# Expert weights split into halves during attention and read back from DRAM, results scattered without addition, experts of the first 512 tokens chosen after the last attention block

## What is computed

```
def _route(x, gate_w, gate_bias):
    scores = sigmoid(x @ gate_w.T)                 # n x 16
    sb = scores + gate_bias
    group_scores = sum of the best 2 of sb in each of 4 groups of 4
    masked = sb where its group is one of the best 2 groups, else -inf
    tidx = the best 4 of masked
    w = scores[tidx] / (sum(scores[tidx]) + 1e-20) * 2.5
combine[n, tidx] = w
hact = silu(x @ w1[e].T) * (x @ w3[e].T) * combine
y = sum over e of hact @ w2[e].T
out = x + tanh(g) * (y + shared expert(x))         # 1024 tokens, experts of 256 x 192
```

## Time and profile before

| | |
|---|---|
| median of 3 runs | 1149.02 us (1147.89 to 1149.88) |
| the profiled execution's own time | 1146.89 us |
| its span, first to last instruction | 1145.1 us |
| granted TensorE clock, mean | 0.955 |
| busy share of the span | PE 86%, DVE 71%, ACT 63%, POOL 37% |
| after the last attention block (from about 921 us) | 224 us |

### The profile page before, as it was taken

How to read it: one execution, slowest core, us unless ns; L and a number is a source line. 1 busy time by engine, 2 the same in 40 slices (tenths; PEclk the granted TensorE clock), 3 DMA queues, 4 the chain that set the end, 5 groups by cost and what they waited for, 6 DMA issues and landing times. The chain is left out here.

```text
span 1145.1 us, 19033 instructions
## 1 busy us (share of the span) xinstructions
PE 988.5 (86%) x6544; PEld 872.5 (76%) x6544; DVE 818.6 (71%) x1655; ACT 723.5 (63%) x1393; POOL 419.6 (37%) x407
## 2 busy tenths in 40 slices
PE   1789989898799989999999999999999868279892
PEld 1668878687688768898888889898888867268882
DVE  6687765777623389897888889887888874666553
ACT  3477756766633478777777878777777743166551
POOL 5164432543167700402022020402017138666663
PEclk9899989999999999999999999999999888589996
DMA  4100000001211399300100001000002114467676
GB/s 132 33 1 1 1 5 1 1 1 38 78 42 35 111 278 281 114 1 2 37 1 1 1 1 38 1 1 2 29 1 69 48 41 143 137 162 129 104 116 139
DMA packets 70767, 67.51 MB, mean 59 GB/s; under 512 B 15505, under 2 KB 67985, under 8 KB 70161
## 3 DMA queue, kind: packets, MB, share of 16 engines
q1 hardware_dynamic: 62368, 55.66, 17.5%
q0 software_dynamic: 8304, 10.64, 5.7%
HBM read 34.20 MB, written 32.07 MB: 58 GB/s over the span
## 5 line engine op out<-in xcount | busy, mean ns | idle before, releaser
L337 PE MATMUL PS<-R 128*128 128x512 f32 (+3 forms) x2669 | 576.4, 360 | 44.3 <-POOL R L562 8.2
L337 PEld LDWEIGHTS PS<-R 128*128 128x128 f32 x2669 | 429.4, 195 | 102.2 <-issue 23.5
L1713 DVE TENSOR_TENSOR R<-PS,R 128x512 fp32r<-128x512 f32 x320 | 205.0, 682 | 40.0 <-ACT R L1366 39.1
L1366 ACT ACTIVATE R<-PS 128x512 fp32r<-128x512 f32 x320 | 174.6, 596 | 79.8 <-PE PS L812 78.6
L1329 ACT ACTIVATE FA<-PS,nmax 128x1024 f32<-128x1024 f32 (+1 forms) x160 | 192.6, 1204 | 34.7 <-DVE nmax L1702 18.0
L825 PE MATMUL PS<-R 128*128 128x256 f32 x1408 | 203.7, 290 | 12.0 <-DVE FB L1721 10.7
L812 PE MATMUL PS<-eye,FA 128*128 128x128 f32 x1408 | 185.5, 276 | 12.5 <-DVE R L1713 4.2
L825 PEld LDWEIGHTS PS<-R 128*128 128x128 f32 x1408 | 179.7, 191 | 20.0 <-issue 17.3
L812 PEld LDWEIGHTS PS<-eye,FA 128*128 128x128 f32 x1408 | 161.2, 141 | 44.1 <-issue 19.6
L1702 DVE TENSOR_REDUCE nmax<-PS 128x1 f32<-128x1024 f32 x128 | 155.5, 1220 | 33.3 <-PE PS L337 22.9
L520 POOL TENSOR_SCALAR R<-R 64x512 fp32r<-64x512 f32 x40 | 25.8, 646 | 318.9 <-ACT R L1481 259.0
(11 more groups left out here) (249 smaller groups left out, 1240.0 us busy)
## 6 DMA issues: line engine op xcount, KB each, us to landing
rows<-xs SPq DMA_DIRECT2D x3, 5869.5 KB, 45.6
FA<-rows SPq DMA_DIRECT2D x47, 136.5 KB, 2.6
wst<-w_in SPq DMA_DIRECT2D x4, 1024.0 KB, 5.1
wst<-we_in SPq DMA_DIRECT2D x16, 256.0 KB
wst<-we_in SPq DMA_DIRECT2D x24, 128.0 KB
sums<-xs SPq DMA_DIRECT2D x2, 1152.0 KB, 23.3
FB<-k_in SPq DMA_DIRECT2D x16, 128.0 KB, 2.0
FA<-sums SPq DMA_DIRECT2D x8, 256.0 KB, 4.6
```

Of the source, the lines that this page charges most:

```text
L337: last = mm(out, a, b, start=(n == 0), stop=(n == len(passes) - 1), skip_group_check=skip)
L1366: a_(L.pt[0][:, (u // 2) % 2, 4 * g_:4 * g_ + 4, (u % 2) * P:(u % 2) * P + P], L.turn(u, g_).rearrange("p (t n) -> p t n", t=4), ACT.Copy) ...
L1713: inc(v.tensor_tensor(lo, turned, hi.bitcast(F32), ALU.subtract), "p_lo")
```

## The change

Four things change.

- **Weights.** During the second attention SP loads each raw expert (5 DMAs), POOL splits it in three pieces (`presplit`, two instructions each) and SP stores the two halves to a DRAM buffer `split_d`; two experts at a time, at fixed places of POOL's program. From the last block on POOL issues one DMA of 128 x 2560 values for each expert (`fetch_expert`), from float32 in DRAM to float32r in `R`, in six groups with a semaphore each. The splits by ACT, POOL and DVE after the attention go.
- **Results.** The weight of a choice is no longer multiplied in before the scatter. Every choice of every token has a DRAM row of its own in `parts_d` (4 x token + choice), so POOL's scatter is a plain one; 4 may be in flight. SP's load of rows no longer waits for it. At the end SP loads all four parts of 128 tokens (8 DMAs of 512 KB), and DVE adds them with their weights, 32 instructions.
- **Choice.** Chunk 0's groups are chosen after the block's outputs are split, its experts after the second sequence's norm; the rest follows with chunk 1, ahead of most of the shared expert.
- **Fill.** The zero rows are written in three parts between the loads of the experts; the two sum buffers are gone.

```diff
-PLANES = 2
+SPARE_ROWS = NB * S * 4
 CHUNKS = ((0, 4), (4, 4))
-SPLIT_POOL = 11
-HI_AT = {1: 9, 2: 10, 4: 11, 6: 12, 8: 13, 10: 14, 12: 15}
-LO_AT = {5: 11, 7: 12, 9: 13, 11: 14, 13: 15}
-LOAD_AT = {3: (9, 10), 7: (11, 12), 9: (13,), 11: (14,), 13: (15,)}
+FETCHED = ((0, 1, 2), (3, 4, 5), (6, 7, 8, 13, 14), (9, 10), (11, 12), (15,))
+FETCHED_IN = {e: i for i, group in enumerate(FETCHED) for e in group}
...
+    raw_gate_up, raw_down = FB[:, 1024:1792], xs[:, 0:512]
+    pieces = [(raw_gate_up[:, 0:512], 6144, 0), (raw_gate_up[:, 512:768], 9216, 512), (raw_down, 6144, 768)]
...
-    sums_d = [nc.dram_tensor(f"sums{i}", (NB * S + P, D), F32, kind="Internal").ap() for i in range(PLANES)]
+    parts_d = nc.dram_tensor("parts", (SPARE_ROWS + 48 * P, D), F32, kind="Internal").ap()
+    split_d = nc.dram_tensor("split", (E, P, WX), F32, kind="Internal").ap()
...
+        def stage_expert(e):
+            m, h = e // 2, e % 2
+            full, part, c = 2 + 3 * m + 2 * h, 3 + 3 * m, slice(DH * h, DH * h + DH)
+            gate_up = raw_gate_up.rearrange("p (a i) -> p a i", a=4)
+            cols = we_d[:, :, 0:512].rearrange("t p (a i) -> t p a i", a=4)
+            if e == 0:
+                sp.wait_ge(s["xc_lo"], 4)
+            first(sp, "e_split", 3 * e)
+            sp.dma_start(gate_up[:, :, 0:P], cols[full]).then_inc(s["raw_in"], 16)
+            sp.dma_start(gate_up[:, :, P:EI], cols[part][:, :, c]).then_inc(s["raw_in"], 16)
+            sp.dma_start(raw_down[:, 0:256], we_d[full][:, 512:768]).then_inc(s["raw_in"], 16)
+            for rows, _ in halves:
+                sp.dma_start(raw_down[rows, 256:512], we_d[part][c, 512:768]).then_inc(s["raw_in"], 16)
+            for i, (src, at, col) in enumerate(pieces):
+                n = src.shape[1]
+                sp.wait_ge(s["e_split"], 3 * e + i + 1)
+                sp.dma_start(split_d[e].rearrange("p (j c) -> p j c", j=2)[:, :, col:col + n],
+                             R[:, at:at + 2 * n].bitcast(F32).rearrange("p (j c) -> p j c", j=2)).then_inc(s[f"stored{i % 2}"], 16)
...
+        def preset_rows(c):
+            sp.wait_ge(s["preset"], 1)
+            sp.dma_start(rows_d.rearrange("(c p) n -> p c n", p=P)[:, c:c + 43, :],
+                         fill.unsqueeze(1).to_broadcast([P, 43, ROW])).then_inc(s["filled"], 16)
...
+        for g in range(1, NG1):
+            for e in range(4 * g - 2, 4 * g):
+                stage_expert(e)
+            if g < 3:
+                preset_rows(43 * g)
+            for e in range(4 * g, 4 * g + 2):
+                stage_expert(e)
+            if g + 1 < NG1:
+                sp.wait_ge(s["w1o_split"], g + 1)
+                sp.dma_start(wst[:, 0:W1_COLS], w1_d[g + 1]).then_inc(s["w1_in"], 16)
...
-                sp.wait_ge(s[f"sent{j % PLANES}"], 16 * ((j - HELD) // PLANES + 1))
+                sp.wait_ge(s["xt_done"], j - HELD + 1)
+                sp.wait_ge(s["dest_sum"], j - HELD + 1)
...
+        sp.wait_ge(s["weighted"], 1)
+        for r in range(RINGS):
+            sp.wait_ge(s[f"sent{r}"], 16 * len(range(r, TILES, RINGS)))
+        parts = parts_d[0:SPARE_ROWS, :].rearrange("(t p k) n -> t p (k n)", p=P, k=4)
+        for t in range(NB * TT):
+            sp.dma_start(back[t], parts[t]).then_inc(s[f"got{t}"], 16)
...
+        def presplit(e):
+            pool.wait_ge(s["raw_in"], 80 * (e + 1))
+            for i, (src, at, _) in enumerate(pieces):
+                n = src.shape[1]
+                first(pool, f"stored{i % 2}", 16 * (e if i == 1 else 2 * e + i // 2))
+                hi, lo = R[:, at:at + n], R[:, at + n:at + 2 * n]
+                g.tensor_scalar(hi, src, 1.0, 0.0, ALU.mult, ALU.add).then_inc(s["pool_free"], 1)
+                pool.wait_ge(s["pool_free"], 3 * e + i + 1)
+                g.tensor_tensor(lo, src, hi.bitcast(F32), ALU.subtract).then_inc(s["e_split"], 1)
+                pool.wait_ge(s["e_split"], 3 * e + i + 1)
...
+            presplit(4 * i - 2)
+            presplit(4 * i - 1)
...
+        def fetch_expert(e):
+            c = expert_at(e)
+            g.dma_start(R[:, c:c + WX], split_d[e]).then_inc(s[f"weights_in{FETCHED_IN[e]}"], 16)
+        pool.wait_ge(s["pj_done"], 28 * NG1)
         for e in range(3):
-            expert_split(e)
-        pool.wait_ge(s["rbc"], 2 * (2 * NG1 + 2))
-        pool.wait_ge(s["o_sum"], BLOCKS * (2 * NG1 + 2))
-        row_numbers(4, 4)
-        pool.wait_ge(s["at_lo"], 4 + 4 * NG1)
-        for h in range(2):
-            half = before16[:, 128 * h:128 * h + 128]
-            step(g.iota(half.bitcast(I32), [[1, 8], [-1, E]], base=8 * h, channel_multiplier=0))
-            step.wait()
-            step(g.tensor_scalar(half, half.bitcast(I32), 0.0, float(P), ALU.is_gt, ALU.mult))
-        step.wait()
-        pool.sem_inc(s["consts"], 1)
-        expert_lo(3)
-        expert_lo(4)
+            fetch_expert(e)
+        pool.wait_ge(s["scored"], UNITS * (2 * NG1 + 2))
+        for e in range(3, 6):
+            fetch_expert(e)
+        pool.wait_ge(s["pv_done"], BLOCKS * (2 * NG1 + 2))
+        for e in (6, 7, 8, 13):
+            fetch_expert(e)
+        pool.wait_ge(s["wo_done"], 4 + 4 * NG1)
+        fetch_expert(14)
...
         place_rows(0)
-        expert_lo(5)
-        expert_lo(6)
         place_rows(1)
+        pool.wait_ge(s["part_set"], 2)
         g.memset(hrow[:, :, EI:256], 0.0).then_inc(s["hrow_zeroed"], 1)
-        for e in range(7, SPLIT_POOL):
-            expert_lo(e)
+        pool.wait_ge(s["e_y"], 4)
+        for e in range(9, 13):
+            fetch_expert(e)
         for j in range(TILES):
-            plane = j % PLANES
+            r = j % RINGS
+            if j == 8:
+                pool.wait_ge(s["y_done"], 8)
+                fetch_expert(15)
+            pool.wait_ge(s["dest_set"], j + 1)
             pool.wait_ge(s["y_out"], j + 1)
-            if j >= PLANES:
-                pool.wait_ge(s[f"sent{plane}"], 16 * (j // PLANES))
-            g.indirect_dma_start(sums_d[plane],
-                                 bass.IndirectOffsetOnAxis(ap=got[:, j % HELD, ROW - 1:ROW].bitcast(U32), axis=0),
-                                 put[:, j % RINGS, :], None, compute_op=ALU.add).then_inc(s[f"sent{plane}"], 16)
+            if j >= RINGS:
+                pool.wait_ge(s[f"sent{r}"], 16 * (j // RINGS))
+            g.indirect_dma_start(parts_d, bass.IndirectOffsetOnAxis(ap=tile_dest[:, j:j + 1], axis=0), put[:, r, :],
+                                 None).then_inc(s[f"sent{r}"], 16)
...
+            if j < E:
+                group_of = FETCHED_IN[j]
+                pe.wait_ge(s[f"weights_in{group_of}"], 16 * len(FETCHED[group_of]))
...
-                elif u == 16:
-                    choose(0)
             attention(L1, b, C, fill)
             if not more:
                 out_norm(L1, C)
                 out_lo(L1, b, C)
-                find_slots(0)
+                choose_groups(0)
...
         norm(4 * NB + 2, x_tiles(1), late1)
+        choose_experts(0)
+        split_norm(3 * NB + 2, 1)
+        mark_chosen(0)
+        number_rows(0)
+        find_slots(0)
+        find_weights(0)
+        choose_groups(1)
+        choose_experts(1)
+        mark_chosen(1)
+        number_rows(1)
+        find_slots(1)
+        find_weights(1)
         job(0, 0)
         job_low(0, 0)
-        split_norm(3 * NB + 2, 1)
-        choose(1)
         job(1, 1)
-        find_slots(1)
         job_low(1, 1)
-        job(2, 0)
-        job_low(2, 0)
-        job(3, 1)
-        job_low(3, 1)
-        dve.wait_ge(s["consts"], 2)
+        dve.wait_ge(s["ew_split"], 2)
...
+        v.tensor_copy(owned[:, :, E], tile_iota)
+        job(2, 0)
+        job_low(2, 0)
+        do(v.tensor_tensor(owned[:, :, 0:E], owner[:, :, 0:E], owner[:, :, 1:E + 1], ALU.subtract))
+        job(3, 1)
+        job_low(3, 1)
...
-        def expert_lo(e):
-            dve.wait_ge(s["w_hi"], e - 2)
-            r, hi, lo = e % 2, expert_at(e), expert_at(e) + WX // 2
-            v.tensor_tensor(R[:, lo:lo + 768], raw_in[r], R[:, hi:hi + 768].bitcast(F32), ALU.subtract)
-            inc(v.tensor_tensor(R[:, lo + 768:lo + 1280], raw_out[r], R[:, hi + 768:hi + 1280].bitcast(F32), ALU.subtract),
-                "w_dve")
+        def find_shares():
+            total, inverse = bo[:, 200:208], bo[:, 208:216]
+            parts = part_w.rearrange("p (t k) -> p t k", k=4)
+            do(v.tensor_reduce(total, parts, AX.X, ALU.add))
+            do(v.tensor_scalar(total, total, 1e-20, None, ALU.add))
+            do(v.reciprocal(inverse, total))
+            do(v.tensor_scalar(inverse, inverse, 2.5, tg[:, 3:4], ALU.mult, ALU.mult))
+            inc(v.tensor_tensor(weight.rearrange("p (t k) -> p t k", k=4), parts,
+                                inverse.unsqueeze(2).to_broadcast([P, NT, 4]), ALU.mult), "weighted")
...
-            if j in LO_AT:
-                expert_lo(LO_AT[j])
-        for w in range(4):
```

(59 more changed lines are left out.)

233 lines of the change are left out of this document (78 added, 155 removed).

## The result

The changed kernel took **1141.98 us** (median of 6 runs, 1140.45 to 1143.81); the kernel before took 1149.45 in as many runs beside it. The ratio is 0.9929, 95% interval 0.9905 to 0.9954: 8 us faster (5 to 11), where the forecast of 1130 meant 19. The stated range was 1117 to 1150.

A forecast was written before the change was run, and what follows sets the result against it. It took the attention as PE-bound and the tiles as held by the pair of adds. Terms 0 − 24.4 + 1.5 − 4.5 + 9.1 = −18.3 gave span 1126.8, 1130.7 on the median's scale, told as 1130; range 1117 to 1150.

The forecast's parts named there:

- Part 2: Tile stage: sums' waits and splits between tiles go, PE sets the pace at 2.12 us a tile; −24.4 us.
- PE's floor of 2.08 us: Tile stage: spacing of two PE row turns where nothing was late, against 2.67 us each in the kernel before.
- what holds it is the pair of adds: Tile stage before: POOL waits 1.79 us for an earlier add; ACT and SP wait for the same landings.
- Parts 4 and 5: Kernel's end: last scatter's way to the return's loads −4.5 us; return with 4 MB instead of 2, +9.1 us.
- Part 6: Attention: presplits fit in POOL's room, 10 to 12 us each, the fill stays under the attention; 0 us.
- Cover that holds: Attention: query copies and low parts of keys queued behind presplits stay covered unless presplit DMAs take over twice the estimate.
- The mechanism stood among the rivals: Attention: POOL's presplit subtractions slow DVE beside them, late query copies hold PE; 10 to 20 us, 1140 to 1150, chance 0.06.
- Part 1: From the choice to the first tiles: earlier choice, last placement stays, net start of tiles 0 us, −4 to +4.
- Gathers of the first tiles run beside the fetches: +1.5: Start of the tiles: the first tiles' row gathers share time with expert fetches, costing 1.5 us.
- −1.5 for `owned`: Start of the tiles: `owned` splits in two, its first piece not waiting for placed rows; −1.5 us on tile 0's first product.
- Part 3: POOL's queue in the tiles: scatter 0 stands behind fetches 9 to 12, so `rows_out` of tile 4 waits; +1.5 us.
- rival of a slow fetch: POOL's queue: fetches into float32r run like the adds, 11.5 us each, delaying placements and scatters; 1201 us, chance 0.15.

The follow-up runs named there:

- E8: Changed kernel with adding scatters in place of plain ones, only two in flight, target zero-filled by SP: 1163.06 us (one run); tile 2 to 46 took 102.4 us.
- E1: Changed kernel, with POOL waiting ahead of each pair of presplits until DVE has split the ended block's output: 1135.76 us, 0.9877 of before.
- E4: Kernel before, plus six unused POOL copies and subtractions at each of six block ends of the second attention, no DMA added: 1156.13 us, 1.0063 of before.
- E2: Changed kernel, with POOL waiting until PE has turned tile 1's rows before issuing the fetches of experts 9 to 12: 1135.21 us, 0.9881 of before.
- E5: Changed kernel with chunk 0's choice put back in the last attention block, its slots behind the output split: 1131.21 us, 0.9843 of before.
- E3: Changed kernel with both waits, presplits behind the block's output split and fetches 9 to 12 behind tile 1: 1129.48 us, 0.9833 of before.

## Why the prediction was right or wrong

- **Part 2, the tiles: right in size, in part for another reason.** −25.6 against −24.4, and PE's floor of 2.08 us holds to the end. But "what holds it is the pair of adds" is shown for 6.4 us only (E8); half of the gain is in the first fourteen tiles, where POOL's low parts of experts held the first add itself. Part 2 takes these splits away too, but counts nothing for them.
- **Parts 4 and 5, the end: right.** −4.0 against −4.5 and +8.2 against +9.1. DVE's 32 instructions run at 0.50 us each, as said, and the loads are hidden beside them:

```profile
1124.05 7.99 DVE L2235 SCALAR_TENSOR_TENSOR x<-FA,rr,x 128x256 f32<-128x256 f32 x16 [8.21 <-DMA FA<-parts]
```

- **Part 6, the attention: 0 forecast, +7.9 measured, one of the two large errors.** "Cover that holds" was counted for late query copies, and PE waited for none. The presplits ran where they were allowed to, which was beside L1754, and cost 6 x 1.31 = 7.9 us there (E1 takes it away, E4 makes it alone). The mechanism stood among the rivals, with L2159 against L2164 as evidence, and was given 0.06. Its price doesn't follow from its rows: a tenth of L2159's loss (5.2 − 0.95 us) in each of 8 blocks is 3.4 us, not 10 to 20. That the result lies in its 1140 to 1150 is chance: 7.9 us alone would have made 1138, and the loss at the first loads came on top. The step that was missing is small: to look, at the place where POOL becomes free, for what DVE does there. Two DVE instructions that read SBUF twice stand there, with others behind them that PE waits for.

  The Trainium skill, "SBUF — State Buffer", section on the two sides of SBUF, states the rule: a VectorE instruction with two SBUF inputs and a GpSimd instruction that reads SBUF lock one another out for the whole instruction, and so do a VectorE instruction in a 2-port perf mode and any GpSimd instruction. The trace agrees for the first kind, 2.60 against 1.29 us, and so it does on the other side: DVE's instructions that read PS took 1.09 us for three in both kernels. E1's instructions of the norm, with one tensor in SBUF, were held too; whether they ran in such a mode no run shows.
- **Part 1, the tiles' start: wrong in one term.** "Gathers of the first tiles run beside the fetches: +1.5", and with −1.5 for `owned` 0 from the last placement to the tiles; +7.9 measured. E2 puts the term itself at 9: without the fetches tile 2 follows the last placement by 9.9 us instead of 18.9. The prediction followed the four fetches only in POOL's own queue, to the scatters behind them; what they hit first was another queue's loads. The other terms of the part held: 41.5 us for the placements against 41, −4.5 for the choice, and about −0.8 for `owned` and what goes with it (9.9 in E2 against 10.7 before).
- **Part 1, what the choice is worth: right in its sum of 0, and too narrow.** The last placement did move only as the attention moved it. E5 shows that this part of the change loses 9 us of placement time which the former order would have kept once POOL splits no experts between the two runs.
- **Part 3, the stall of scatters: right as 0 or little.** No scatter waited for the fetches in the changed kernel; POOL's first scatter waited 22 us for ACT. That is luck in part: the tiles were late because of the same fetches. 5.46 MB of POOL's queue took 81.1% of 18 us, 374 GB/s, T = 3.5 us: at the lower end, and below the 4.8 taken. The rival of a slow fetch (T = 11.5) is refuted: a conversion to float32r on the way shows no price beside the 360 GB/s of the plain placements. In E3, where the fetches move behind the loads, the stall appears with 1.4 us.

Sum: forecast −18.3. The start of the tiles, forecast 0, is 18.3 us late in the profiled pair: 7.9 at the block ends, 7.9 at the first loads, 1.3 that were there ahead of the second attention, and 1.2 in small pieces on the way to the last placement. The other parts came out 3.1 better than forecast (tiles 1.2, stall 1.5, the end 0.3). −18.3 + 18.3 − 3.1 = −3.1. Two terms failed, then, part 6's cover and part 1's loads beside fetches, and each is shown by a run that takes it away (E1, E2).
